# Two graph transformer layers on one core: the scores and the similarity of two half steps in one stretch of TensorE

## What is computed

```python
h = relu(layernorm(x))
m = h @ map_w.T + map_b                      # 8 heads of 64 channels
n = m / |m|                                  # per head
similar = (n @ n.T > 0.1)                    # cosine similarity of nodes
q, k = m @ q_w.T + q_b, m @ k_w.T + k_b
p = softmax(q @ k.T / 8, masked by adj)
a = similar * p
x = x + relu((a @ v @ gcn_W.T) / (a.sum(-1) + 1))
```

## Time and profile before

| | |
|---|---|
| median of three runs | 2648.26 us |
| the profiled execution, its own time | 2644.7 us |
| its span | 2642.9 us |
| TensorE busy | 2584.8 us, 98% |
| VectorE busy | 1991.5 us, 75% |
| ScalarE busy | 1754.2 us, 66% |
| GpSimd busy | 1400.6 us, 53% |

### The profile page before, as it was taken

How to read it: one execution, slowest core, us unless ns; L and a number is a source line. 1 busy time by engine, 2 the same in 40 slices (tenths; PEclk the granted TensorE clock), 3 DMA queues, 4 the chain that set the end, 5 groups by cost and what they waited for, 6 DMA issues and landing times. The chain is left out here.

```text
span 2642.9 us, 62516 instructions
## 1 busy us (share of the span) xinstructions
PE 2584.8 (98%) x20882; PEld 1392.6 (53%) x20886; DVE 1991.5 (75%) x6361; ACT 1754.2 (66%) x5020; POOL 1400.6 (53%) x2790
## 2 busy tenths in 40 slices
PE   7999999999999999999999999997999999999998
PEld 3455555555555555555555555554555555555554
DVE  6577777777877777777777777786777777777766
ACT  3566666666666666666666666675777777777774
POOL 5254455455554555455545554544565656565552
PEclk9999999999999999999999999998999999999999
DMA  4367676666676667767676676678787777778764
GB/s 142 74 150 157 131 143 142 143 150 131 140 151 142 132 136 149 150 131 138 145 148 136 132 145 151 139 149 191 155 175 162 168 165 168 164 162 169 161 148 104
DMA packets 945488, 387.43 MB, mean 147 GB/s; under 512 B 857616, under 2 KB 859152, under 8 KB 945168
## 3 DMA queue, kind: packets, MB, share of 16 engines
q1 hardware_dynamic: 945168, 383.44, 68.5%
HBM read 114.86 MB, written 67.11 MB: 69 GB/s over the span
## 5 line engine op out<-in xcount | busy, mean ns | idle before, releaser
L552 ACT ACTIVATE probs<-probs,negmax 128x128 f32<-128x128 f32 x1024 | 398.2, 390 | 455.0 <-DVE negmax L124 455.0
L465 POOL TENSOR_TENSOR o_sb<-o_sb,xres 128x512 f32<-128x512 f32 x127 | 161.4, 1271 | 498.3 <-DVE o_sb L744 494.9
L166 PE MATMUL l_ps_pj<-hT,room 128*128 128x512 f16 x1488 | 345.3, 382 | 3.0 <-ACT room L1350 3.0
L166 PE MATMUL ps_pj<-wm_hi,hT 128*128 128x512 f16 x1024 | 325.2, 379 | 4.1 <-DVE m_sb L687 3.8
L166 PE MATMUL ps_pj<-wv_hi,hT 128*128 128x512 f16 x1024 | 326.4, 380 | 0.0
L166 PE MATMUL ps_pj<-hT,wk_hi 128*128 128x512 f16 x1024 | 305.9, 380 | 0.9 <-DVE wk_lo L766 0.9
L166 PE MATMUL ps_pj<-hT,wq_hi 128*128 128x512 f16 x1024 | 304.5, 379 | 0.0
L1364 ACT ACTIVATE l_probs<-l_probs,l_negmax 128x128 f32<-128x128 f32 x512 | 199.2, 390 | 139.5 <-DVE l_negmax L124 139.4
L1299 POOL TENSOR_TENSOR l_h<-l_h 128x512 f16<-128x512 f32 x120 | 139.6, 1164 | 282.1 <-DVE l_out_sb L1447 244.9
L124 DVE CUSTOM_DVE_ANT_0 probs<-ps_sc,mask 128x128 f32<-128x128 f32 x1024 | 235.2, 284 | 46.9 <-PE ps_sc L986 46.3
L726 DVE SCALAR_TENSOR_TENSOR c<-cprobs,c 128x512 f16<-128x512 f32 x256 | 185.3, 724 | 79.6 <-ACT c L559 79.1
(11 more groups left out here) (172 smaller groups left out, 6197.2 us busy)
## 6 DMA issues: line engine op xcount, KB each, us to landing
xg<-in_x SPq DMA_DIRECT2D x128, 256.0 KB, 3.5
xres<-in_x SPq DMA_DIRECT2D x128, 256.0 KB, 3.2
x_scratch<-o_sb SPq DMA_DIRECT2D x128, 256.0 KB, 2.4
out<-l_out_sb SPq DMA_DIRECT2D x128, 256.0 KB, 3.3
l_ring<-x_scratch SPq DMA_DIRECT2D x124, 256.0 KB, 3.2
mask_u<-in_adj SPq DMA_DIRECT2D x64, 64.0 KB, 2.6
cpT<-c SPq DMA_TRANSPOSE x256, 3.2
xg<-x_scratch SPq DMA_DIRECT2D x12, 256.0 KB, 3.7
```

The source lines that it names most:

```text
L166: last = pe.matmul(out, a(kt), b(kt), start=(n == 0), stop=(n == 3 * kts - 1))
L465: nc.gpsimd.tensor_tensor(o_sb[:, j % 2], o_sb[:, j % 2], xres[:, j % 2], ALU.add).then_inc(res_done, 1)
L552: last = nc.scalar.activation(probs[:, i], probs[:, i], ACT.Exp, bias=negmax[:, u % 2, i:i + 1], scale=-1.0, accum_out=zsum[:, u % 4, hh:h ...
```

## The change

In layer 0, `scores` is cut in three functions: `score_inputs` (the waits), `products` (the fp32 matmuls) and `similarity` (the fp16 matmuls). In every even step of the groups 0 to 30 `scores_of_two(n + 1)` makes both the block of step n + 1 and that of step n + 2, in the order products, products, similarity, similarity. In the odd steps no block is left. `scores(0)` at the start and the last group (`last_group`) are as before. The other engines' programs, the PSUM tiles and layer 1 are unchanged.

```diff
-            def scores(n):
+            def score_inputs(n):
                 t, u = divmod(n, 8)
                 j, half = u // 2, u % 2
-                cols = slice(j * P, (j + 1) * P)
                 if u < 2:
                     pe.wait_ge(q_done, count(QUAD * t + 2 * u + 2))
                     pe.wait_ge(k_done, count(QUAD * t + 2 * u + 2))
...
                 pe.wait_ge(negmax_done, count(n - 1))
                 pe.wait_ge(cp_done, count(n - 1))
+
+            def products(n):
...
+            def similarity(n):
...
                 mm.then_inc(s_ready, 1)
+
+            def scores(n):
+                score_inputs(n)
+                products(n)
+                similarity(n)
+
+            def scores_of_two(n):
+                score_inputs(n)
+                products(n)
+                score_inputs(n + 1)
+                products(n + 1)
+                similarity(n)
+                similarity(n + 1)
...
-                    scores(n + 1)
+                    if u % 2 == 0:
+                        scores_of_two(n + 1)
```

More of the change, by code:

```diff
@@ L974, in scores @@
                 pe.wait_ge(cp_done, count(n - 1))
+            def products(n):
+                t, u = divmod(n, 8)
+                j, half = u // 2, u % 2
+                cols = slice(j * P, (j + 1) * P)
                 for pl in range(2):
```

## The result

| | before | after |
|---|---|---|
| median of the runs beside each other | 2648.83 us (4 runs, 2646.65 to 2649.66) | 2676.44 us (4 runs, 2671.35 to 2677.36) |
| ratio | | 1.0105 [1.0092, 1.0117] |
| the profiled execution, its own time | 2644.7 us | 2675.95 us |
| its span | 2642.9 us | 2674.2 us |

The change makes the kernel 1.05% slower, 27.6 us by the medians and 31.3 by the two profiled spans. The forecast was 2640 with a range up to 2653: the sign was wrong. Layer 1 takes nearly the same in both: from TensorE's last matmul of layer 0 (it starts at 1796.07 before and at 1828.24 after) to the end it is 846.9 us before and 845.9 after.

What follows compares the result with a forecast made beforehand. TensorE was taken to set the time of layer 0. The terms -36 + 29.5 - 3 + 1.5 = -8 us took the profiled 2644.7 to 2636.7, or 2640 us at the median; the range was 2617 to 2653.

Steps and rivals of the forecast that it cites:

- Edges removed: TensorE, groups 0 to 30: 124 entries and exits of blocks fewer, 0.29 us each, -36 us.
- The new wait at step 0: TensorE's second products wait for VectorE's selection at step 0, 0.95 us in each of 31 groups, +29.5 us.
- the 0.6 of the upper bound: Step 0: the x transfer comes 0.6 us later against TensorE in all groups, for a mean wait of 1.04 us.
- Step 6 does not wait: Step 6: VectorE's selection ends 0.7 us before the second products need it, so no wait there.
- A wait that goes: Step 1: TensorE's wait for step 0's late `m_copy` disappears, -3 us.
- The chain itself: VectorE and ScalarE in step 4: the shift from the shorter step 3 is mostly hidden, 0.05 us per group, +1.5 us.
- the upper bound that I had stated: Step 4: one more collision of VectorE with GpSimd, 0.7 to 0.9 us, partly covered.
- (d): Steps 4 or 5: one more uncovered VectorE and GpSimd collision, 0.7 us per group, delays steps 6 and 0; 2660 us, chance 0.10.
- (e): Second products: only a drain goes, the entry's weight load is paid again, 124 x 0.1 = 12 us; 2652 us, chance 0.03.
- What would show it: Profile after: 112 weight loads behind "issue", steps of 5.56 and 7.42 us, selection waits at step 0 only, about 0.9 us each.

Runs made afterwards that it cites:

- e2_pairs_0_6: The kernel after the change, but with pairs at steps 0 and 6 alone, the other steps with their own block: 2655.02 us, ratio 1.0028.
- e9_after_residual_late: The kernel after the change, with GpSimd's residual of step 3 moved behind the last `v_low`: 2631.32 us, ratio 0.9941.
- the best kernel: The kernel after, with the fourth graph's statistics behind step 0's selection and GpSimd's step 3 residual behind the last `v_low`: 2606.0 us, 0.9844 of the kernel before.
- e1_pairs_2_4: The kernel after the change, but with pairs at steps 2 and 4 alone, the other steps with their own block: 2656.92 us, ratio 1.004.
- e4_after_lows_late: The kernel after the change, with VectorE's `h_low` and `n_low` moved behind `p_low` and the row maxima of the same step: 2694.9 us, ratio 1.018.

## Why the prediction was wrong

Step by step, as the prediction has them:

- *Edges removed*, -36 us: **right**. Steps of 5.55 and 7.42 where 5.56 and 7.42 were forecast, and 33.8 us by experiment. In the profile after there are 142 weight loads behind "issue" and not 112: besides one per pair there is about one per group behind a wait.
- *The new wait at step 0*, +29.5: the mechanism was right, the size was not. Over the 31 groups it is about 40 us of waiting and some 3 more at the restart. TensorE restarts 0.15 us behind the selection, as the row of before had it. The x transfer is 1.1 us later against TensorE at the group shown (0.42 ahead of the block's start before, 0.71 behind it now), not the 0.6 of the upper bound. I had taken the slip from TensorE's edges alone. On the mean of 26 groups the selection ends 0.99 behind the block's first instruction before and 1.73 after; it is 1.33 in `e2_pairs_0_6`, where step 4 has no slip, and 1.12 in `e9_after_residual_late`, where the collision is gone.
- *Step 6 does not wait*: **wrong**, +18 us. The 0.7 us to spare were read rightly, but the selection came 1.04 later against the block (0.14 ahead of it, now 0.90 behind).
- *A wait that goes*, -3: right in kind (0.6 us of waits are left); with step 1 back at its plain length it is 0.19 x 31 = 6 us.
- *The chain itself*, +1.5, 0.05 us per group: **this is the step that failed**. I wrote that `h_low` and `n_low` "both end late for GpSimd's sake, not for ScalarE's, so most of the 0.7 is hidden". It was no cover. GpSimd's instruction moved along (1041.49 to 1058.13 is 1.46 to 2.24 behind the step's start), so the collision moved with the chain and grew: 0.36 came through and 0.42 were added. (ScalarE's `h_high` was 0.49 later against the step, where I had 0.7.) The slip was 0.78, near the upper bound that I had stated and then discounted.
- *The rivals*: (d) is what happened, with the place, the price per group (0.7 against 0.78) and the two steps that it named, and it had a chance of 0.10. Its threshold, a slip of 0.3 us, was passed in every group, not in some. Its time of 2660 was 16 us short: the waits of steps 0 and 6 came to 63 us and not to 51, and the 8 us of the clock were not in it. (e), the entry paid again, does not happen in a stream (pairs without a wait are 0.55 apart, 1.16 us for 16 passes) but does, with about 0.1 us, where TensorE had to wait between the two products.
- *What would show it*: "waits at steps 2, 4 or 6 would mean (d)". They did.

The later start of `h_low` is not GpSimd's: it stayed at 2.27 in the kernel without the collision, and went back to 1.91 when the pairs were taken out.

## What to carry to other kernels

A gain read from the edges of the busiest engine's stream was right to a few us, and still the time went up: shortening the steps of the leading engine moves it against every chain that runs at its own pace, so the place to price is the spare time of each wait on the far side of those chains, first of all where two other engines collide. An instruction that is late because another engine is in its way has no slack for that; a shift ahead of it is hidden only if what is in its way stays where it is. And before such a change is dropped, look at what stands ahead of the late producer in its own queue: here one GpSimd and one VectorE instruction group in other places turned +1.05% into -1.56%, while without the change the same two moves give 0.3%.

## What the runs showed of the hardware

**VectorE beside GpSimd.** `h_low` (two inputs in SBUF) takes 0.69 us alone and 1.39, 1.80 or 1.81 beside GpSimd's `tensor_tensor`, by how much of it overlaps; over 200 to 1700 us its mean is 964 ns after the change and 689 in the best kernel. The selection, whose similarity comes from PSUM, took 0.74 beside `v_low` (1057.12), and after the change all 256 of them lie between 0.72 and 0.75. What GpSimd pays differs: after the change all its residuals take 1.26 to 1.28, the one beside `h_low` too, while without the collision at `h_low` one beside `p_low` takes 1.71. The Trainium skill (SBUF — State Buffer, Who interferes with whom) says that a VectorE instruction with two SBUF inputs contends with a GpSimd instruction that reads SBUF, since its second input takes the shared read interface, while one with at most one SBUF input does not (it makes an exception of VectorE's 2-port modes). The durations agree for `h_low`, and for the selection too, one of whose two large inputs lies in PSUM. By that rule the prediction could have expected that a shift which leaves the two side by side is paid and not hidden.

**The clock.** After the change there are five short stretches in layer 0 in which the granted clock is about half (the 1.2 GHz level); between 29 and 1771 us the kernel before has none. The trace of after, one of them, as windows (PE busy, and so on; the granted clock is the third from the end) and as a timeline:

```profile
1141.20:1144.60 3.40, 3.40 (x29) 1.81 (x26) 2.06 (x10) 1.69 (x9) 2.54 (x11) 0.53 0.56 131
```

```profile
1140.42 0.73 PE L983 MATMUL ps_sc<-room 64*128 64x128 f32 x8 [1.71 <-DVE cprobs L720]
1140.94 1.50 PE L994 MATMUL ps_sc<-space 64*128 64x128 f16 x24
```

The 24 similarity matmuls take 1.50 us in place of 0.84. Each of the five stretches follows a wait at step 0 of 1.83 us or more, counted as the distance between the two products less the 0.55 that it has without a wait, which is 0.16 more than the idle time in the profile's rows. Nine groups have such a wait and four of them keep the full clock, one with 2.43 us, as long as the longest of all. No shorter wait in this kernel was followed by one. In `e1_pairs_2_4` two stretches follow idle times of 2.13 and 2.04 us and none follows one of 2.86; in `e4_after_lows_late` one follows 2.15 and none 1.92 or 1.93. So a long wait can cost the clock here and need not; what decides is open. The best kernel has no such stretch between 18 and 1751 us. I had priced a wait at its own length. Two groups with the same wait of 2.43 have a step 0 of 11.59 with a stretch and 9.95 without, two with 2.04 one of 11.20 and 9.56: each stretch costs 1.6 us on top, about 8 us in all, a quarter of the loss.
